# Attention outputs turned in 32-wide blocks on VectorE, with output weights laid out to match

## The chip, the cores and the metric

The kernel runs on one core of a Trainium2 chip. The metric is the device time of one execution in microseconds (us). The engines are TensorE (PE; its weight loads are shown as PEld), VectorE (DVE), ScalarE (ACT), GpSimd (POOL) and SyncE (SP), which mostly issues DMAs.

## What is computed

A transformer layer on x of shape (8, 256, 512), all in f32. `_layernorm` normalises rows; 32 query heads of width 16 share 8 key/value heads, so a *group* is 4 query heads with their key/value head.

```python
B, T, HID, H, HK, D = 8, 256, 512, 32, 8, 16
q = heads(concat([ctx, ln(x)]) @ Wq, 32)
kcat = concat([ctx @ Wsk, ln(x) @ Wk]); vcat = concat([ctx @ Wsv, ln(x) @ Wv])
scores = q @ kcat.T / sqrt(D) + alibi      # each token sees the 64 before it, twice
o = softmax(scores) @ vcat                 # per head, D = 16
x = x + tanh(g_xattn) * (o.reshape(B, T, HID) @ Wo)
n = ln(x)
# feed-forward: router softmax, top 4 of 128, experts as mixtures of 8 bases,
# and a shared gated product
x = x + tanh(g_ffn) * ffn(n)
```

## The kernel before

Every f32 operand of a large product is split into a high and a low part of type fp32r, and a product is three passes (hi x hi, lo x hi, hi x lo; `PASSES`, `product` at L1509).

Attention is software-pipelined over slots. A slot `n` is one block of 64 queries of one group of one batch: 4 blocks (NB) x 8 groups (HK) = 32 slots a batch (UNITS), 256 slots (END) in all and 38 more that drain the pipeline. Each engine's program is a loop over the slots, in which offsets (L75 to L82) say how many slots after its own first slot a piece of work is done: `due(n, offset)` for work once a batch, `group_due(n, offset)` for work once a group. The order on each engine is fixed by hand; engines meet at semaphores.

In slot n TensorE computes the scores of slot n (`scores`, L1594, into one of two banks; it waits until VectorE has the maxima of slot n-2), then the turned scores of slot n-14 (`scores_turned`, L1615; ScalarE takes their exponentials, L867). VectorE takes the row maxima (`maxima`, L1180). Once a group TensorE turns the maxima's halves (`turn_max`, L1605), which ScalarE copies and sends into the query stack by a DMA.

With the values (`times_v`, L1628) come 128 rows by 256 tokens in `PO`: for each of 4 heads 32 rows, of which 16 are the output and 16 hold the sum of exponentials (the values are followed by ones). Then:

- ScalarE copies `PO` to `OS` (`pv_out`, L875), which frees `PO` for the next group.
- TensorE turns `OS` in two 128x128 turns (`turn_o`, L1639) into `PN`: tokens by (head, 32).
- VectorE takes the reciprocal of the sums (L1196) and multiplies (L1200) into `O`, rows of tokens by 512 (`norm`). It stands before the slot's maxima.
- Once a batch, TensorE turns `O` back in 2 x 4 turns (`turn_rows`, L1646); ScalarE and VectorE split it into `OT` hi and lo (`rows_high` L881, `rows_low` L1206).
- Two products with Wo (`times_wo`), the residual, statistics (`residual`, L1215 to L1220), roots on GpSimd (`x1_roots`), normalisation (`x1_normalise`, L1226), turns of x (`turn_x`, L1658), and its split (`x_high` L885, `x_low` L1231), which for the first six batches uses the memory of `OT` and is kept in HBM by a DMA (L558).

All projections, turns of inputs, rows, Wo products and turns of x share two PSUM banks (`PJ`) in the order of `projections()` (L122): a job waits until VectorE is done with the job two before it (`take_bank`). In slots modulo 32 the jobs stand at: inputs 0, 1, 2, 3; K 5, 6; queries 8, 10, 12, 14; turn of V 16; rows 21, 22; Wo 24, 26; V 28, 29; x 31 and 0 (`rows`, `wo` and `x` belong to the batch before). After the 256 slots the first tiles of the feed-forward are interleaved with the drain (`ROUTER_AT`, `SHARED_AT`); the feed-forward follows.

## Time and profile before

| | us |
|---|---|
| median of 3 runs | 999.35 |
| lowest, highest | 998.37, 1000.41 |
| profiled execution | 1003.41 |
| its span, first to last instruction | 1001.6 |
| TensorE busy | 934.7 |
| VectorE busy | 567.5 |
| ScalarE busy | 422.1 |
| GpSimd busy | 369.4 |

The busy times are those of the profiled execution, as the union of an engine's instructions. Matmuls overlap: the duration of one includes its latency, so the time that it takes from the engine is the distance from its start to the next one's. The attention slots run from about 40 to 460 us of the span, the drain to about 535, the feed-forward to the end.

### The profile page before, as it was taken

The page shows a single profiled execution, that of the slowest core. Times are in us where ns is not written, and L with a number is a line of the kernel's source. Part 1 is how long each engine was busy: PE and PEld are TensorE (multiplying, and loading weights), DVE is VectorE, ACT ScalarE, POOL GpSimd, SP SyncE. Part 2 cuts the span into 40 slices and gives each one's busy share as a digit, 9 for nine tenths or more (in the row PEclk, how much of TensorE's full clock was granted, in tenths as well). Part 3 has the DMA queues.
Part 4 walks back from the last instruction along what each step waited for, and adds up shares of the span by engine and source line. Part 5 has one row for each costly group of instructions (what it writes and reads, how often), then busy time and mean ns, then how long its engine had stood idle before and what let it go on. Part 6 is the DMA issues. An engine that isn't in the chain of part 4 may idle for free.

```text
span 1001.6 us, 18083 instructions
## 1 busy us (share of the span) xinstructions
PE 934.7 (93%) x6936; PEld 803.3 (80%) x6936; DVE 567.5 (57%) x1135; ACT 422.1 (42%) x906; POOL 369.4 (37%) x401
## 2 busy tenths in 40 slices
PE   6779999999999999999997988979999999999997
PEld 6668989888888989978786766768888888888876
DVE  5356574856657474666123564566566565565566
ACT  5655454444544444455311423334434444444331
POOL 2020000100000010002000997626687887887730
PEclk9989999999999999989999998989999999999998
DMA  6595566555655554698010104441111211201044
GB/s 219 167 204 154 125 165 162 150 178 137 175 141 162 130 156 124 159 248 255 1 42 1 43 22 156 150 158 41 65 51 39 79 40 45 85 26 59 22 151 185
DMA packets 79559, 117.04 MB, mean 117 GB/s; under 512 B 6249, under 2 KB 49002, under 8 KB 78442
## 3 DMA queue, kind: packets, MB, share of 16 engines
q1 hardware_dynamic: 77744, 115.18, 40.8%
q8 instruction: 56, 0.92, 0.4%
q10 hardware_dynamic: 1730, 0.71, 0.3%
q14 instruction: 29, 0.24, 0.1%
HBM read 77.13 MB, written 37.81 MB: 115 GB/s over the span
## 4 chain that ended last, share of the span: by engine, by line
PE 84%; DVE 7%; DMA 4%; issue 2%; ACT 1%; SPq 1%; POOL 0%; DVEq 0%; ACTq 0%; POOLq 0%
PE ps_proj L1515 21%; PE ps_scores L1840 17%; PE ps_scoresT L1840 9%; PE ps_scores L1515 5%; PE ps_o L1628 5%; PE ps_scoresT L1615 5%; PE ps_scores L1594 4%; PE ps_proj L1840 4%; PE ps_scoresT L1515 4%; PE ps_o_max L1639 2%; DVE neg_max L1180 1%; PE ps_proj L1538 1%; PE ps_o L1515 1%; DMA xn_rows<-in_x 1%; DMA q_kept<-qT_hi 1%
## 5 line engine op out<-in xcount | busy, mean ns | idle before, releaser
L1180 DVE TENSOR_REDUCE neg_max<-ps_scores 128x2 f32<-128x384 f32 (+1 forms) x256 | 130.4, 517 | 127.3 <-PE ps_scores L1594 126.4
L867 ACT ACTIVATE probsT<-ps_scoresT 128x512 f32<-128x512 f32 (+1 forms) x256 | 138.8, 544 | 144.3 <-PE ps_scoresT L1615 140.8
L1071 ACT ACTIVATE part_sums<-ps_scores 128x512 f32<-128x512 f32 x96 | 57.5, 599 | 134.3 <-PE ps_scores L1840 132.4
L1594 PE MATMUL ps_scores<-k_stack,q_stack 114*128 114x192 f32 (+1 forms) x512 | 105.3, 291 | 9.0 <-DVE neg_max L1180 8.1
L1615 PE MATMUL ps_scoresT<-q_stack,k_stack 116*128 116x256 f32 x448 | 105.8, 308 | 6.2 <-DMA q_stack<-max_rows 4.9
L1594 PEld LDWEIGHTS ps_scores<-k_stack,q_stack 114*128 114x128 f32 x512 | 81.7, 197 | 17.0 <-DVE neg_max L1180 12.3
L650 POOL TENSOR_SCALAR var_eps<-mean_var 128x2 f32<-128x2 f32 x8 | 2.1, 261 | 226.9 <-DVE mean_var L1129 226.8
L765 POOL TENSOR_TENSOR big<-big,basis 128x512 f32<-128x512 f32 x56 | 77.5, 1403 | 15.6 <-DVE basis L1469 15.6
L753 POOL TENSOR_TENSOR w_expert_lo<-w_sums,w_expert_hi 128x256 fp32r<-128x256 f32 x64 | 64.2, 1014 | 46.9 <-ACT w_expert_hi L1001 46.9
L1615 PEld LDWEIGHTS ps_scoresT<-q_stack,k_stack 116*128 116x128 f32 x448 | 73.4, 199 | 7.9 <-DMA q_stack<-max_rows 5.3
L1515 PE MATMUL ps_proj<-actT_hi,wq_hi 128*128 128x256 f32 x224 | 65.1, 290 | 0.0
L1628 PE MATMUL ps_o<-probsT,v_ones 128*32 128x128 f32 (+1 forms) x2048 | 64.4, 268 | 0.5 <-issue 0.5
L1515 PE MATMUL ps_proj<-actT_hi,wq_lo 128*128 128x256 f32 x224 | 63.8, 285 | 0.0
L1515 PE MATMUL ps_proj<-actT_lo,wq_hi 128*128 128x256 f32 x224 | 63.8, 285 | 0.0
L650 POOL TENSOR_SCALAR x_var_eps<-x_mean_var 128x2 f32<-128x2 f32 x8 | 2.8, 354 | 161.1 <-DVE x_mean_var L1220 161.1
L1460 DVE TENSOR_TENSOR basis<-part_sums,silu_gate 128x512 f32<-128x512 f32 x32 | 24.0, 751 | 67.2 <-ACT silu_gate L1079 67.2
L1628 PEld LDWEIGHTS ps_o<-probsT,v_ones 128*32 128x32 f32 x2048 | 53.6, 112 | 10.0 <-issue 1.7
L1469 DVE TENSOR_TENSOR basis<-basis,big 128x512 f32<-128x512 f32 x56 | 58.2, 1040 | 1.0
L753 POOL TENSOR_TENSOR w_expert_lo<-w_raw,w_expert_hi 128x256 fp32r<-128x256 f32 x48 | 45.9, 968 | 20.3 <-ACT w_expert_hi L1001 20.2
L1439 DVE TENSOR_TENSOR part_sums<-part_sums,ps_scoresT 128x512 f32<-128x512 f32 x32 | 22.0, 688 | 54.0 <-ACT part_sums L1071 54.0
L1840 PE MATMUL ps_scores<-sum_hi,w_expert_hi 128*128 128x512 f32 x128 | 50.1, 392 | 2.1 <-ACT part_sums L1071 2.1
L1840 PE MATMUL ps_scores<-xnT_hi,w_expert_hi 128*128 128x512 f32 x128 | 49.9, 390 | 1.1 <-DVE x_part L1391 1.1
(264 smaller groups left out, 2571.5 us busy)
## 6 DMA issues: line engine op xcount, KB each, us to landing
k_stack<-k_kept SPq DMA_DIRECT2D x64, 192.0 KB, 5.3
q_stack<-q_kept SPq DMA_DIRECT2D x31, 384.0 KB, 5.4
q_kept<-qT_hi SPq DMA_DIRECT2D x16, 512.0 KB
big<-coeff_rows SPq DMA_DIRECT2D x8, 1024.0 KB, 4.7
xn_rows<-in_x SPq DMA_DIRECT2D x8, 512.0 KB, 4.0
k_kept<-kT_hi SPq DMA_DIRECT2D x16, 256.0 KB
q_kept<-qT_lo SPq DMA_DIRECT2D x8, 512.0 KB
x_rows<-in_x SPq DMA_DIRECT2D x8, 512.0 KB, 5.1
```

The source lines that it names most:

```text
L753: pool.tensor_tensor(WS[n % 2]["lo"][:, w, :], w_source(n, w), WS[n % 2]["hi"][:, w, :].bitcast(F32), ALU.subtract).then_inc(e_lo, 1)
L765: pool.tensor_tensor(dst, dst, BS[:, j, :], ALU.add).then_inc(acc_done, 1)
L867: act.activation(PT[:, g % 2, 2 * j:2 * j + blocks].rearrange("p h f r w -> p (h f r w)"), ST[:, n % 2, 0:blocks].rearrange("p h n -> p (h ...
L1071: act.activation(TP[:, u % 2, j, :], src[:, u % 2, :], ACT.Copy).then_inc(taken, 1)
L1180: dve.tensor_reduce(NM[:, g % 2, 2 * i:2 * i + 2], SA[:, n % 2, :, 0:keys], AX.X, ALU.max, negate=True).then_inc(max_done, 1)
L1460: dve.tensor_tensor(BS[:, j, :], up, silu, ALU.mult).then_inc(e_prod, 1)
L1469: dve.tensor_tensor(dst, BS[:, j, :], cB[:, k % 2, group_columns(t)], ALU.mult).then_inc(basis_done, 1)
L1515: ins = pe.matmul(out, stat(s, c), mov(m, c), start=c == cs[0] and j == 0, stop=c == cs[-1] and j == PARTS - 1)
L1594: ins = pe.matmul(SA[:, n % 2, f, 0:2 * (near.stop - near.start)], QS[0:TOP, g, i, f].rearrange("p r w -> p (r w)"), keys[:, near, :].rear ...
L1615: ins = pe.matmul(ST[:, n % 2, v, :], KS[0:ROWS, g, j + v, 1 - v].rearrange("p w s -> p (w s)"), QS[0:ROWS, g, j + v].rearrange("p f r w - ...
L1628: ins = pe.matmul(PO[32 * r:32 * r + 2 * D, j * W:j * W + cols_j], VA[:, j, g, :], PT[:, n % 2, 2 * j:2 * j + cols_j // W, :, r, :].rearra ...
L1840: ins = pe.matmul(bank[:, u % 2, :], WS[n % 2][s][:, w, c * P:(c + 1) * P], operand(MEETS[w], m, c, g), start=first and c == 0 and j == 0, ...
```

## The change

PO is turned by VectorE itself, straight out of PSUM, in 32x32 blocks (`o_turn`): the 32 rows of a head and 32 tokens become 32 tokens by 32. In that form it takes the reciprocal and multiplies; the 16 values of two neighbouring groups (an even and an odd one) are laid side by side, and at the odd one a second 32x32 turn brings them back as (head, group parity, 16) by tokens, `OR`. ScalarE and VectorE split `OR` into `OT` (`o_high`, `o_low`), once a pair of groups. The turns on TensorE (`turn_o`, `turn_rows`), the copy `pv_out` and the split of the rows are gone. `times_v` waits for VectorE's turn. The rows of Wo are permuted before the launch to match. x gets buffers of its own (`XS`; its low half is kept by two DMAs instead of one). `o_turn` stands behind the slot's maxima.

The jobs modulo 32 are now: inputs 0 to 3; K 5, 6; queries 8, 10, 13, 16; turn of V 15; Wo 20, 23; V 25, 27; x 30, 31. The last router product is in slot 33 of the drain instead of 34.

```diff
@@ -73,13 +73,12 @@
...
-NM_TURN, PV, PV_OUT, TURN_O, NORM = 6, LAG + 5, LAG + 6, LAG + 9, LAG + 10
-TURNS_BETWEEN = (TURN_O - NM_TURN) // NB
+NM_TURN, PV, O_TURN, O_HIGH, O_LOW = 6, LAG + 5, LAG + 6, LAG + 7, LAG + 8
...
-PREP, K_PROJ, Q_PROJ, V_PROJ = (-32, -31, -30, -29), (-27, -26), (-24, -22, -20, -18), (-4, -3)
+PREP, K_PROJ, Q_PROJ, V_PROJ = (-32, -31, -30, -29), (-27, -26), (-24, -22, -19, -16), (-7, -5)
...
-TURN_V, TURN_ROWS, TIMES_WO, TURN_X = 16, (53, 54), (56, 58), (63, 64)
-LOAD_X1, X1_ROOTS, X1_NORMALISE, KEEP_X = 42, 59, (62, 63), 67
+TURN_V, TIMES_WO, TURN_X = 15, (52, 55), (62, 63)
+LOAD_X1, X1_ROOTS, X1_NORMALISE, KEEP_X = 42, 57, (60, 61), 66
@@ -114,7 +113,7 @@
...
-ROUTER_AT = {0: 0, 4: 1, 12: 2, 34: 3}
+ROUTER_AT = {0: 0, 4: 1, 12: 2, 33: 3}
@@ -164,11 +163,13 @@
...
-    O = at("o_rows", 192 * KIB, [P, TB, HID])
-    OS = at("oT_sums", 196 * KIB, [P, T])
+    OB = at("o_blocks", 192 * KIB, [P, T // 32, 2 * D])
+    ON = at("o_normal", 193 * KIB, [P, 2, T // 32, 2 * D])
+    OR = at("oT_raw", 195 * KIB, [P, 2, T])
...
+    XS = {"hi": at("xs_hi", 216 * KIB, [P, HC, T], F32R), "lo": at("xs_lo", 208 * KIB, [P, TB, HC, P], F32R)}
@@ -554,9 +554,10 @@
...
-                for j, h in enumerate(("hi", "lo")):
-                    sp.dma_start(xT_kept_d[b, j].rearrange("p c n -> p (c n)"),
-                                 OT[h][:, :, :, :].rearrange("p t c n -> p (t c n)").bitcast(F32)).then_inc(xT_kept, 16)
+                sp.dma_start(xT_kept_d[b, 0].rearrange("p c n -> p (c n)"),
+                             XS["hi"][:].rearrange("p c n -> p (c n)").bitcast(F32)).then_inc(xT_kept, 16)
+                for t in range(TB):
+                    sp.dma_start(xT_kept_d[b, 1][:, :, t * P:(t + 1) * P], XS["lo"][:, t].bitcast(F32)).then_inc(xT_kept, 16)
@@ -868,20 +869,18 @@
...
-        def pv_out(n):
-            act.wait_ge(pv_mm, n + 1)
-            if n >= 1:
-                act.wait_ge(o_turned, n)
-            act.activation(OS[:], PO, ACT.Copy).then_inc(oT_out, 1)
-        def rows_high(b, t):
-            act.wait_ge(oT_mm, TB * b + t + 1)
-            if t == 0 and 1 <= b <= SPILLED:
-                act.wait_ge(xT_kept, 32 * b)
-            act.activation(OT["hi"][:, t], chunks(place("rows", b, t)), ACT.Copy).then_inc(oT_hi, 1)
+        def o_high(p):
+            b, c = divmod(p, HC)
+            act.wait_ge(o_back, p + 1)
+            if c == 0 and b >= 1:
+                act.wait_ge(wo_mm, TB * b)
+            act.activation(OT["hi"][:, :, c, :], OR[:, p % 2, :].rearrange("p (t n) -> p t n", t=TB), ACT.Copy
+                           ).then_inc(oT_hi, 1)
...
         def x_high(b, t):
...
+            if t == 0 and 1 <= b < SPILLED:
+                act.wait_ge(xT_kept, 48 * b)
...
         def split_hi(idx, used=None):
@@ -1189,22 +1185,30 @@
...
-        def norm(n):
-            b, g = divmod(n, HK)
+        def o_turn(n):
+            p, odd = divmod(n, 2)
+            dve.wait_ge(pv_mm, n + 1)
+            if n >= 1:
+                dve.wait_ge(o_done, n)
+            dve.transpose(OB[:].rearrange("p k e -> p (k e)"), PO).then_inc(o_turned, 1)
...
-            v = PN.rearrange("p (t r e) -> p t r e", t=TB, r=G)
-            dve.reciprocal(RI[:], v[:, :, :, D]).then_inc(inv_done, 1)
-            if g == 0 and b >= 1:
-                dve.wait_ge(oT_mm, TB * b)
+            dve.reciprocal(RI[:], OB[:, :, D]).then_inc(inv_done, 1)
...
-            dve.tensor_tensor(O[:, :, g * G * D:(g + 1) * G * D].rearrange("p t (r d) -> p t r d", r=G),
-                              v[:, :, :, 0:D], RI[:].unsqueeze(3).broadcast_to([P, TB, G, D]),
-                              ALU.mult).then_inc(o_done, 1)
-        def rows_low(b, t):
-            dve.wait_ge(oT_hi, TB * b + t + 1)
-            dve.tensor_tensor(OT["lo"][:, t], chunks(place("rows", b, t)),
-                              OT["hi"][:, t].bitcast(F32), ALU.subtract).then_inc(pj_done, 1)
+            dve.tensor_tensor(ON[:, p % 2, :, odd * D:(odd + 1) * D], OB[:, :, 0:D],
+                              RI[:].unsqueeze(2).broadcast_to([P, T // 32, D]), ALU.mult).then_inc(o_done, 1)
+            if odd:
+                dve.wait_ge(o_done, n + 1)
+                if p >= 2:
+                    dve.wait_ge(oT_lo, p - 1)
+                dve.transpose(OR[:, p % 2, :], ON[:, p % 2].rearrange("p k e -> p (k e)")).then_inc(o_back, 1)
+        def o_low(p):
+            c = p % HC
+            dve.wait_ge(oT_hi, p + 1)
+            dve.tensor_tensor(OT["lo"][:, :, c, :], OR[:, p % 2, :].rearrange("p (t n) -> p t n", t=TB),
+                              OT["hi"][:, :, c, :].bitcast(F32), ALU.subtract).then_inc(oT_lo, 1)
...
         def residual(b, t):
@@ -1223,6 +1227,8 @@
...
+            if t == 0 and 1 <= b <= SPILLED:
+                dve.wait_ge(xT_kept, 48 * b)
@@ -1269,11 +1275,14 @@
...
-            m = group_due(n, NORM)
-            if m is not None:
-                norm(m)
+            m = group_due(n, O_LOW)
+            if m is not None and m % 2:
+                o_low(m // 2)
...
+            m = group_due(n, O_TURN)
+            if m is not None:
+                o_turn(m)
@@ -1600,8 +1606,6 @@
...
-            if n > TURNS_BETWEEN:
-                pe.wait_ge(o_done, n - TURNS_BETWEEN)
...
         def scores_turned(n):
@@ -1621,7 +1625,7 @@
...
-                pe.wait_ge(oT_out, n)
+                pe.wait_ge(o_turned, n)
@@ -1630,25 +1634,9 @@
...
-        def turn_o(n):
-            pe.wait_ge(oT_out, n + 1)
-            if n >= 1:
-                pe.wait_ge(o_done, n)
-            pe.wait_ge(nm_out, min(n + TURNS_BETWEEN + 1, GROUPS))
-            for t in range(TB):
-                ins = pe.transpose(PN[:, t * P:(t + 1) * P], OS[:, t * P:(t + 1) * P], ident[:])
-            ins.then_inc(o_turned, 1)
-        def turn_rows(b, t):
-            dst = take_bank("rows", b, t)
-            pe.wait_ge(o_done, HK * (b + 1))
-            for c in range(HC):
-                ins = pe.transpose(dst[:, c * P:(c + 1) * P], O[:, t, c * P:(c + 1) * P], ident[:])
-            ins.then_inc(oT_mm, 1)
         def times_wo(b, t):
...
-            pe.wait_ge(pj_done, passed("rows", b, t))
+            pe.wait_ge(oT_lo, HC * (b + 1))
...
         def turn_x(b, t):
@@ -1927,6 +1908,8 @@
...
+    heads = inputs["L0_xattn_Wo"].reshape(HK // 2, 2, G, D, HID)
+    inputs["L0_xattn_Wo"] = np.asarray(heads).transpose(0, 2, 1, 3, 4).reshape(HID, HID)
```

## Rows read from the trace of the kernel before

**Rows 1.** Page, part 1: engine, busy us (share of the span), instructions.

```profile
PE 934.7 (93%) x6936; PEld 803.3 (80%) x6936; DVE 567.5 (57%) x1135; ACT 422.1 (42%) x906; POOL 369.4 (37%) x401
```

**Rows 2.** Timeline, TensorE: start, us, engine, line, operation, tiles; where slots and K begin.

```profile
256.28 0.42 PE L1594 MATMUL ps_scores<-k_stack,q_stack 114*128 114x128 f32 x2
...
265.42 0.35 PE L1515 MATMUL ps_proj<-actT_hi,wkv_hi 128*128 128x256 f32 x1 [0.70 <-DVE actT_lo L1145]
...
297.04 0.42 PE L1594 MATMUL ps_scores<-k_stack,q_stack 114*128 114x128 f32 x2
...
305.67 0.42 PE L1594 MATMUL ps_scores<-k_stack,q_stack 114*128 114x128 f32 x2
...
312.11 0.42 PE L1594 MATMUL ps_scores<-k_stack,q_stack 114*128 114x128 f32 x2
...
369.52 0.42 PE L1594 MATMUL ps_scores<-k_stack,q_stack 114*128 114x128 f32 x2
```

**Rows 3.** Groups by line and form, TensorE: records, busy us, mean ns, idle before.

```profile
L1639 PE MATMUL ps_o_max<-ident,oT_sums 128*128 128x128 f32 x128 | 28.2, 302 | 0.0
```

**Rows 4.** Timeline, TensorE, same columns: prices from start to start.

```profile
293.90 0.63 PE L1646 MATMUL ps_proj<-ident,o_rows 128*128 128x128 f32 x4
294.29 0.45 PE L1594 MATMUL ps_scores<-k_stack,q_stack 114*128 114x192 f32 x2
...
295.94 0.97 PE L1628 MATMUL ps_o<-probsT,v_ones 128*32 128x128 f32 x32
296.84 0.44 PE L1639 MATMUL ps_o_max<-ident,oT_sums 128*128 128x128 f32 x2
...
297.58 0.40 PE L1515 MATMUL ps_proj<-wo_hi,oT_hi 128*128 128x512 f32 x1
...
300.35 0.37 PE L1594 MATMUL ps_scores<-k_stack,q_stack 114*128 114x192 f32 x2
...
306.21 0.28 PE L1515 MATMUL ps_proj<-actT_hi,wkv_hi 128*128 128x256 f32 x1
...
307.65 0.37 PE L1594 MATMUL ps_scores<-k_stack,q_stack 114*128 114x192 f32 x2
...
308.00 0.28 PE L1515 MATMUL ps_proj<-actT_hi,wkv_hi 128*128 128x256 f32 x1
```

**Rows 5.** Groups by line and form, VectorE: same columns.

```profile
L1200 DVE TENSOR_TENSOR o_rows<-ps_o_max,inv_sums 128x128 f32<-128x128 f32 x64 | 18.7, 292 | 2.7
...
L1157 DVE TENSOR_TENSOR qT_lo<-ps_proj,qT_hi 128x256 fp32r<-128x256 f32 x28 | 11.6, 416 | 3.7 <-ACT qT_hi L847 3.7
```

**Rows 6.** Timeline, VectorE: the start behind the scores, and the residual.

```profile
300.75 0.56 DVE L1180 TENSOR_REDUCE neg_max<-ps_scores 128x2 f32<-128x384 f32 x1 [2.22 <-PE ps_scores L1594]
301.23 0.74 DVE L1215 SCALAR_TENSOR_TENSOR x_rows<-ps_proj,tanh_gates,x_rows 128x512 f32<-128x512 f32 x1
...
302.83 0.53 DVE L1180 TENSOR_REDUCE neg_max<-ps_scores 128x2 f32<-128x384 f32 x1
```

**Rows 7.** Timeline, VectorE, light groups of the last batch.

```profile
434.18 0.21 DVE L1196 RECIPROCAL inv_sums<-ps_o_max 128x8 f32<-128x8 f32 x1 [0.97 <-PE ps_o_max L1639]
...
434.63 0.41 DVE L1180 TENSOR_REDUCE neg_max<-ps_scores 128x2 f32<-128x256 f32 x1
...
437.89 0.21 DVE L1196 RECIPROCAL inv_sums<-ps_o_max 128x8 f32<-128x8 f32 x1 [0.97 <-PE ps_o_max L1639]
```

**Rows 8.** Timeline, TensorE: a turn of inputs that waited in slot 1.

```profile
373.32 0.66 PE L1538 MATMUL ps_proj<-ident,ctx_rows 128*128 128x128 f32 x4 [1.11 <-DVE actT_lo L1145]
```

**Rows 9.** Windows: us, busy of each engine (count), PEclk, DMA share, GB/s.

```profile
370.00:374.00 4.00, 2.34 (x19) 1.91 (x19) 3.16 (x8) 2.52 (x6) 0.00 (x0) 0.99 0.10 17
374.00:378.00 4.00, 4.00 (x46) 3.57 (x46) 2.31 (x4) 2.54 (x5) 0.00 (x0) 0.58 0.78 302
```

**Rows 10.** Timeline, TensorE: the turns of x after the last batch.

```profile
528.23 1.08 PE L1658 MATMUL ps_proj<-ident,x_normal 128*128 128x128 f32 x8 [1.40 <-DVE x_normal L1226]
```

More of the change, by code:

```diff
@@ L127, in projections @@
     kinds = [("prep", PREP, 2), ("k", K_PROJ[1:], 2), ("q", Q_PROJ, 1), ("v", V_PROJ[1:], 1), ("turn_v", (TURN_V,), 0),
-             ("rows", TURN_ROWS, 0), ("wo", TIMES_WO, 0), ("x", TURN_X, 0)]
+             ("wo", TIMES_WO, 0), ("x", TURN_X, 0)]
     for n in range(SLOTS):
@@ L225, in build @@
     gates, tg = little("gates", [P, 2]), little("tanh_gates", [P, 2])
-    RI = little("inv_sums", [P, TB, G])
+    RI = little("inv_sums", [P, T // 32])
     amp, amp2, mix = little("amp", [P, KB, 2]), little("amp2", [P, KB]), little("mix", [P, KB])
@@ L243, in build @@
     PNM = ps("ps_o_max", [P, 2, T])
-    PO, PN, PM = POB[:, 0, :], PNM[:, 0, :], PNM[0:4 * NB, 1, 0:P]
+    PO, PM = POB[:, 0, :], PNM[0:4 * NB, 1, 0:P]
     PG = SA[:, :, :, :].rearrange("p s h n -> p s (h n)")
@@ L265, in build @@
         sem("s_mm"), sem("max_done"), sem("nm_hi"), sem("nm_lo"), sem("nm_t"), sem("nm_out"))
-    st_mm, exp_done, pv_mm, oT_out, o_turned, inv_done, o_done = (
-        sem("st_mm"), sem("exp_done"), sem("pv_mm"), sem("oT_out"), sem("o_turned"), sem("inv_done"), sem("o_done"))
-    oT_mm, oT_hi, wo_mm, x1_st, x1_ag, x1_rt, x1_n = (
-        sem("oT_mm"), sem("oT_hi"), sem("wo_mm"), sem("x1_st"), sem("x1_ag"), sem("x1_rt"), sem("x1_n"))
+    st_mm, exp_done, pv_mm, o_turned, inv_done, o_done, o_back = (
+        sem("st_mm"), sem("exp_done"), sem("pv_mm"), sem("o_turned"), sem("inv_done"), sem("o_done"), sem("o_back"))
+    oT_hi, oT_lo, wo_mm, x1_st, x1_ag, x1_rt, x1_n = (
+        sem("oT_hi"), sem("oT_lo"), sem("wo_mm"), sem("x1_st"), sem("x1_ag"), sem("x1_rt"), sem("x1_n"))
     xT_mm, xT_hi, x1_kept, xT_kept = sem("xT_mm"), sem("xT_hi"), sem("x1_kept"), sem("xT_kept")
@@ L361, in xT_place @@
         if b < SPILLED:
-            return OT[h][:, :, :, :].rearrange("p t c n -> p (t c n)").rearrange(
-                "p (c t n) -> p c t n", c=HC, t=TB)[:, :, t, :]
+            return XS[h][:, :, t * P:(t + 1) * P] if h == "hi" else XS[h][:, t]
         return XT[h][:, :, (b * TB + t) * P:(b * TB + t + 1) * P]
@@ L568, in _ @@
                 sp.wait_ge(pj_done, passed("v", B - 1, 0))
-                sp.wait_ge(xT_kept, 32 * (m + 1))
+                sp.wait_ge(xT_kept, 48 * (m + 1))
                 sp.dma_start(XT[("hi", "lo")[j]][:, :, m * T:(m + 1) * T].bitcast(F32), xT_kept_d[m, j]).then_inc(xT_in[m // 2], 16)
@@ L947, in _ @@
             for t in range(TB):
-                b = due(n, TURN_ROWS[t] + 1)
-                if b is not None:
-                    rows_high(b, t)
                 b = due(n, TURN_X[t] + 1)
@@ L970, in _ @@
                 act.activation(tg[:], gates[:], ACT.Tanh).then_inc(tg_done, 1)
-            m = group_due(n, PV_OUT)
-            if m is not None:
-                pv_out(m)
+            m = group_due(n, O_HIGH)
+            if m is not None and m % 2:
+                o_high(m // 2)
             s = n - (END - UNITS)
             if s == 18:
-                split_hi(0)
+                split_hi(0, (xT_kept, 48 * SPILLED))
             if s == 20:
@@ L1271, in _ @@
         for n in range(SLOTS):
-            m = group_due(n, NORM)
-            if m is not None:
-                norm(m)
+            m = group_due(n, O_LOW)
+            if m is not None and m % 2:
+                o_low(m // 2)
             if n < END:
                 maxima(n)
+            m = group_due(n, O_TURN)
+            if m is not None:
+                o_turn(m)
             for i in range(4):
@@ L1294, in _ @@
             for t in range(TB):
-                b = due(n, TURN_ROWS[t] + 1)
-                if b is not None:
-                    rows_low(b, t)
                 b = due(n, TIMES_WO[t] + 1)
@@ L1726, in _ @@
                 times_v(m)
-            m = group_due(n, TURN_O)
-            if m is not None:
-                turn_o(m)
             for i in range(4):
@@ L1752, in _ @@
                 turn_v(b)
-            for t in range(TB):
-                b = due(n, TURN_ROWS[t])
-                if b is not None:
-                    turn_rows(b, t)
             for t in range(TB):
```

## Prediction, before the result was known

> **What bounds the kernel now.** I read the page's busy times first: TensorE is busy 93% of the span, VectorE 57%, ScalarE 42% [rows 1]. That is an average, so I went on to the timeline of TensorE's instructions in the attention stage (40 to 505 us), where the change lies. Each slot there starts with the scores matmuls of L1594, so their starts are the slot clock, and a batch is 32 slots. In batch 4 (counted from 0) slots 0 to 4 and the head of 5 take 9.14 us (256.28 to 265.42), slots 5 to 23 take 31.62, slots 24 to 27 take 8.63, slots 28 to 31 take 6.44: together 55.83 us [rows 2]. I split the batch there because three of the four stretches have different limits. The groups by form name what is removed: the turns of L1639 have 128 records, 28.2 us of busy time [rows 3]. A busy time isn't a price here, as matmuls overlap. The price is the distance to the next start.
>
> **What the change takes from TensorE.** A pair of turns (L1639) holds it from 296.84 to 297.04, 0.20 us; four turns of rows (L1646) from 293.90 to 294.29, 0.39 us [rows 2, 4]. There are 64 pairs and 16 fours: 12.8 + 6.2 = 19.0 us. That is the most that TensorE alone can give back, and it counts only where TensorE sets the pace.
>
> **What it adds to VectorE.** Before, a group of heads costs a reciprocal and a product, 0.45 us from start to the next instruction (434.18 to 434.63) [rows 7], and 16 subtractions for the rows. After, a group costs a turn of 128x256 out of PSUM, the reciprocal, the product, and each second group another turn back; each pair of groups also a 128x256 subtraction. No turn on VectorE is in the trace. The nearest row is the 128x256 subtraction out of PSUM, 416 ns [rows 5]; the turn also moves 256 elements per partition. Its bounds: below, 0.20 us, what the product of half the width needs before the next starts (0.292 us long [rows 5]); above, twice the subtraction, 0.83. I take 0.42, and 0.45 where the next waits for it. An even group is then 0.45 + 0.45 = 0.90 us. An odd one must let the product end (0.12 more) and adds 0.33 for the turn back: 1.35. It is placed behind the slot's own maxima, and queued behind it on VectorE are the low halves of projections, the residual, the halves of the maxima, and the next maxima, for which the scores two slots on wait. ScalarE loses a 128x256 copy per group and the rows' copies and gains one copy per pair; it is under half busy and I cost it at nothing, with its slots' exponentials as cover.
>
> The Trainium skill, VectorE: DVE Perf Modes, "The three transpose paths", gives 311 ns for VectorE's 128x128 in blocks of 32 against 390 ns for TensorE's. By those figures TensorE's pair would be 0.78 us and the change would gain about 0.1 us a group even if VectorE were the bound; this trace has 0.20 us for the pair from start to start, so the page's durations are no exchange rate here.
>
> **The sum, batch by batch.** Prices in TensorE's time [rows 4]: a slot of scores and turned scores 0.54 (305.67 to 306.21) or 0.35 where only one turned block is due (307.65 to 308.00); 0.90 more with the values (295.94 to 296.84); a K or V half 1.44 (306.21 to 307.65), so a query part 2.88; a pass through Wo 2.77 (297.58 to 300.35). On average four bare slots are 2.8 with the values.
> Slots 5 to 23 afterwards: 4 fours 11.2, slots 6 and 7 1.95, K 2.88, four query parts 11.5, the turn of V 0.39, two passes of Wo that came from slots 24 and 26 5.54: 33.5. VectorE falls behind a little at slots 19, 20 and 23 (slot 16 has an odd group, the values' copy and statistics): 0.9. So 34.4, from 31.62.
> Slots 24 to 27: after the scores of 24 VectorE starts 0.40 later (300.35 to 300.75) and does maxima 0.34, an odd group 1.35, the residual with its statistics 1.60 (301.23 to 302.83) [rows 4, 6], halves 0.34, and only then the maxima of slot 25, 0.56. Scores of slot 27 can't start before 4.6; slot 27 itself is 1.44 + 1.44. In all 7.5, from 8.63. V now sits there, Wo doesn't.
> Slots 28 to 31: VectorE does maxima, an even group, the copy of V, a normalisation and the halves before TensorE can turn the first block of x: 3.2 us after the scores of 28. Then 0.39, and slot 31 with values and the second turn 1.8. In all 5.3, from 6.44.
> Slots 0 to the K half in 5: one projection a slot over two banks; now x's last low half (0.60) is behind an odd group, so the second turn of the inputs waits until about 3.0 us after the scores of 0; slots 2 and 3 cost 1.1 and 1.9; slot 4 has an even group ahead of the last low half, so K starts 1.8 after slot 5's scores; today TensorE already idles 0.70 before it (the row at 265.42) [rows 2]. In all 8.9, from 9.14.
> Sum 34.4 + 7.5 + 5.3 + 8.9 = 56.1 against 55.83: the 2.4 us that TensorE loses in work come back as waits for VectorE. Six batches: +1.8.
> The last batch has no projections. Its light groups take 3.71 us (434.18 to 437.89) with VectorE waiting 0.97 of them [rows 7]. There the chain runs maxima, scores, values, scores, maxima. The norm's 0.45 leaves it and 0.90 or 1.35 enters: some 4.1 and 4.5. Five such groups: +3.0; elsewhere in that batch three pairs and one set of rows are saved: -1.4. After it, where TensorE runs the shared products: four pairs 0.8, the last rows 0.8, and the wait of 1.40 for the normalised x [rows 10], which now has two shared tiles ahead of it instead of one: -3.0. First batch: -0.2. Total +1.8 + 1.6 - 3.0 - 0.2 = +0.2 us. The profiled execution is 1003.41 us with a span of 1001.6; it would be 1003.6. The shown runs have a median of 999.35, 4.1 below it, so I predict 999.6.
> On SP's queue the queries' store moves two slots later (-16 to -14 before the batch), the first read of them, at -10, waits for it, and they are used at slot 0: ten slots hide it, and without them it would be one landing. The x blocks get places of their own and one more DMA in 512-byte rows for six batches; queued behind it there are stacks that are fetched 14 slots ahead, so nothing. If that cover failed it would be one landing per batch, some 4 us in all.
>
> **Rivals.** (1) VectorE's extra work stays hidden. For it: it's idle 43% of the time, and the one-job-a-slot spread breaks the chain in which TensorE waited 1.11 us for a low half in slot 1 [rows 8]. If half of the 19.0 us stays, 990; if all of it, 980. Against it: the waits computed above at slots 27, 30 and 1. (2) More slow clock. In 370 to 374 us TensorE was busy 2.34 of 4 us, and in the next four the granted clock was 0.58, near the lower of its levels, 1.2 GHz [rows 9]. Such a batch took 57.41 us (312.11 to 369.52) against 55.83 [rows 2], so 1.6 us each, and it's not in every batch. The new waits spread over slots 24 to 5 and are longer in total, some 6 us; if three or four more of them fall, that is 5 to 6 us: 1005. It decides from the point where stretches around slot 1 are as empty as this one. The Trainium skill, TensorE: Matmul & The Clock Gate, Part 1, says that the array is run at half rate after idleness; the two rows agree. (3) The turn of four-byte data costs twice: 0.41 more each, six turns on the path of a batch, 2.5 us; with the last batch +16, of which some hides: 1012. Against it: every other pass over 256 elements takes about 0.42. (4) The change doesn't give TensorE time at all, because the turns that go were in gaps that stay (at the end, too, where the 3.0 us of the sum would then not come): 999.35 + 0.2 + 3.0, so 1002.5. Against it: between 295.94 and 297.04 TensorE goes from the values to the turns to the scores with no idle time noted [rows 2, 4].
>
> **How the numbers follow.** The forecast, stretched to whatever ends within 0.2% (2 us, about what a measurement of this kernel can tell from none), 0.32. (1) 0.31, with anything else that ends below that. (2) 0.20, (3) 0.10, (4) 0.07. Faster 0.31, same 0.32, slower 0.37. The range leaves out the far end of (1), where over half of the 19.0 us stays, and that of (3): 988 to 1011. Cases of both signs hold most of it; the likeliest one's own range is 997 to 1002.
>
> **What would show it.** The turn of 128x256 at 0.42 us on VectorE. A batch without slow clock at 55 to 57 us from scores to scores. TensorE waiting for maxima at slot 27 (over 1 us), for the normalised x at slot 30, for a low half at slot 1, and for VectorE before K. Light groups of the last batch at 4.1 and 4.5 us. VectorE's busy time up by about 64 x 0.42 + 32 x 0.42 + 32 x 0.42 less 11, some 43 us. Wrong if light groups stay at 3.7, or if batches come in at 53 us: then VectorE isn't in the way; or at 59, then a turn costs more than I took.

## The result, and the profile after

The changed kernel takes 1019.26 us (median of four runs, 1013.49 to 1023.81); the kernel before, in the same series, 998.86. The ratio is 1.019, interval 1.0147 to 1.0232: slower by 19 to 20 us. I had forecast 999.6, with a range up to 1011. The profiled execution of after is 1018.43 us, its span 1016.6. The one of before was among its longer ones (1003.41 against a median of 999.35), so the traces show 15.0 of these 20 us.

The page's busy line of after, as in [rows 1]:

```profile
PE 927.8 (91%) x6744; PEld 789.7 (78%) x6744; DVE 604.3 (59%) x1247; ACT 409.5 (40%) x858; POOL 369.9 (36%) x401
```

TensorE has 192 matmuls fewer and is busy 6.9 us less, VectorE 36.8 us more. VectorE's new groups by line and form, against [rows 3, 5]:

```profile
L1195 DVE STREAM_TRANSPOSE o_blocks<-ps_o 128x256 f32<-128x256 f32 x64 | 28.2, 440 | 9.8 <-PE ps_o L1632 9.8
...
L1199 DVE TENSOR_TENSOR o_normal<-o_blocks,inv_sums 128x128 f32<-128x128 f32 x64 | 18.7, 292 | 2.2
...
L1205 DVE STREAM_TRANSPOSE oT_raw<-o_normal 128x256 f32<-128x256 f32 x32 | 14.3, 445 | 1.1
L1210 DVE TENSOR_TENSOR oT_lo<-oT_raw,oT_hi 128x256 fp32r<-128x256 f32 x32 | 13.2, 412 | 2.5 <-ACT oT_hi L877 2.5
```

The turn takes 0.44 us; I had taken 0.42. The whole of an even group holds VectorE for 0.92 us (375.25 to 376.17), that of an odd one for 1.40 (367.56 to 368.96), where I had 0.90 and 1.35. So the prices were right. Now the slot clock, as in [rows 2]: starts of TensorE's scores in batch 5 of after (slots 0, 24, 28, and 0 of the next), and its K half.

```profile
322.62 0.42 PE L1600 MATMUL ps_scores<-k_stack,q_stack 114*128 114x128 f32 x2
...
325.53 0.66 PE L1544 MATMUL ps_proj<-ident,ctx_rows 128*128 128x128 f32 x4 [1.43 <-DVE xs_lo L1237]
...
331.78 0.36 PE L1521 MATMUL ps_proj<-actT_hi,wkv_hi 128*128 128x256 f32 x1 [1.50 <-DVE actT_lo L1141]
...
366.84 0.34 PE L1600 MATMUL ps_scores<-k_stack,q_stack 114*128 114x128 f32 x2
...
370.97 0.28 PE L1609 MATMUL ps_o_max<-ident,max_halves 128*16 128x128 f32 x1 [1.25 <-DVE max_halves L1185]
...
374.53 0.34 PE L1600 MATMUL ps_scores<-k_stack,q_stack 114*128 114x128 f32 x2
...
377.64 0.28 PE L1609 MATMUL ps_o_max<-ident,max_halves 128*16 128x128 f32 x1 [1.23 <-DVE max_halves L1185]
...
380.08 0.42 PE L1600 MATMUL ps_scores<-k_stack,q_stack 114*128 114x128 f32 x2
```

This batch, in which no slow clock falls, takes 57.46 us; the like one before took 55.83 [rows 2]. TensorE has less to do in it and waits four times for VectorE: for x's low half before the turn of the inputs in slot 1, for the last low half before K, and twice for the halves of the maxima (slots 26 and 30). These last waits are the new ones. All waits of TensorE over 0.15 us in this batch (total us, times, longest):

```profile
PE ps_o_max L1609 <- DVE max_halves L1185: 2.5, 2, 1.3
PE ps_proj L1521 <- DVE actT_lo L1141: 1.5, 1, 1.5
PE ps_proj L1544 <- DVE xs_lo L1237: 1.4, 1, 1.4
PE ps_scores L1600 <- DVE neg_max L1176: 0.6, 2, 0.4
```

Together 6.0 us; in the like batch before they are 3.0 (0.55 before the second turn of x in slot 0, 1.11 in slot 1, 0.70 before K, 0.68 before the scores of slot 19). Outside these waits TensorE takes 52.8 us of the batch before and 51.5 after, 1.3 less, where the turns that are gone had been priced at 2.4.

TensorE's waits in the whole execution, before and then after (same columns):

```profile
PE ps_scores L1594 <- DVE neg_max L1180: 8.1, 16, 1.3
PE ps_proj L1538 <- DVE actT_lo L1145: 6.7, 8, 1.1
...
PE ps_o_max L1605 <- DVE max_halves L1189: 3.0, 1, 3.0
```

```profile
PE ps_o_max L1609 <- DVE max_halves L1185: 22.5, 20, 2.2
PE ps_proj L1521 <- DVE actT_lo L1141: 10.5, 7, 1.5
PE ps_proj L1544 <- DVE xs_lo L1237: 7.1, 5, 1.4
PE ps_scores L1600 <- DVE neg_max L1176: 7.0, 22, 1.3
```

What stands ahead of the halves is seen in VectorE's timeline, slot 24 of the same batch:

```profile
368.27 0.29 DVE L1199 TENSOR_TENSOR o_normal<-o_blocks,inv_sums 128x128 f32<-128x128 f32 x1
368.60 0.45 DVE L1205 STREAM_TRANSPOSE oT_raw<-o_normal 128x256 f32<-128x256 f32 x1
368.96 0.71 DVE L1219 SCALAR_TENSOR_TENSOR x_rows<-ps_proj,tanh_gates,x_rows 128x512 f32<-128x512 f32 x1
369.71 0.69 DVE L1222 BATCH_NORM_STATS2 x_stats<-x_rows 128x6 f32<-128x512 f32 x1
370.44 0.18 DVE L1224 BATCH_NORM_AGGREGATE x_mean_var<-x_stats 128x2 f32<-128x6 f32 x1
370.53 0.15 DVE L1183 CAST max_halves<-neg_max 128x8 fp32r<-128x8 f32 x1
370.72 0.19 DVE L1185 TENSOR_TENSOR max_halves<-neg_max,max_halves 128x8 fp32r<-128x8 f32 x1
370.83 0.55 DVE L1176 TENSOR_REDUCE neg_max<-ps_scores 128x2 f32<-128x384 f32 x1
```

Turn, reciprocal, product and turn back, then the residual with its statistics, then the halves, and only then the maxima of slot 25. VectorE has no gap from the maxima of slot 24 (367.22) to those of slot 25. It is 3.99 us from the scores of slot 24 to the maxima of slot 25 (366.84 to 370.83). TensorE's own work covers 2.88 of them (slots 24, 25 and the scores of 26, up to 369.72, where its wait of 1.25 begins).

Where the 15.0 us of span went, from the starts of the scores: first batch +1.1; batch 1 +4.4 (53.88 to 58.29); the next five +6.9; the last batch, from its first to its last scores, +6.4 (39.72 to 46.13); from there to the end -3.8 (535.9 to 532.1). The last batch also runs into the slow clock, one window of it:

```profile
446.00:450.00 4.00, 4.00 (x34) 3.34 (x36) 2.81 (x9) 2.33 (x5) 0.00 (x0) 0.50 1.09 318
```

The granted clock (column before the last two) is 0.50, the lower of the two levels.

Over the whole execution the mean granted clock is 0.971 before and 0.966 after. With two levels that is 58 us at the lower one before and 69 after. What they cost is an estimate: a batch before whose mean is 0.97 takes 1.6 us more than one at 1.00, so a microsecond at the lower level costs about half of one. The 11 more are then worth about 5 of the 15.0 us.

### The profile page after: what moved, and what is told of

Same layout as the page of the kernel before. It is cut to its first block, busy times and chain, and to the rows that moved or that the text cites. A ratio compares the mean times of both kernels' runs of the same rounds, so it can differ in the third digit from the quotient of the medians.

```text
span 1016.6 us, 17719 instructions
## 1 busy us (share of the span) xinstructions
PE 927.8 (91%) x6744; PEld 789.7 (78%) x6744; DVE 604.3 (59%) x1247; ACT 409.5 (40%) x858; POOL 369.9 (36%) x401
## 4 chain that ended last, share of the span: by engine, by line
PE 78%; DVE 13%; issue 3%; DMA 3%; ACT 1%; SPq 1%; POOL 0%; DVEq 0%; POOLq 0%; ACTq 0%
PE ps_proj L1521 19%; PE ps_scores L1821 17%; PE ps_scoresT L1821 9%; PE ps_o L1632 6%; PE ps_scores L1521 5%; PE ps_scores L1600 5%; PE ps_proj L1821 4%; PE ps_scoresT L1521 4%; PE ps_scoresT L1619 4%; DVE o_blocks L1195 2%; DVE neg_max L1176 2%; PE ps_o L1521 1%; DMA xn_rows<-in_x 1%; DVE actT_lo L1141 1%; PE ps_proj L1544 1%
## 5 line engine op out<-in xcount | busy, mean ns | idle before, releaser
L868 ACT ACTIVATE probsT<-ps_scoresT 128x512 f32<-128x512 f32 (+1 forms) x256 | 135.2, 542 | 148.4 <-PE ps_scoresT L1619 146.4
L1632 PE MATMUL ps_o<-probsT,v_ones 128*32 128x128 f32 (+1 forms) x2048 | 67.7, 277 | 0.5 <-issue 0.5
L1632 PEld LDWEIGHTS ps_o<-probsT,v_ones 128*32 128x32 f32 x2048 | 56.2, 116 | 10.6 <-issue 2.4
L1445 DVE TENSOR_TENSOR part_sums<-part_sums,ps_scoresT 128x512 f32<-128x512 f32 x32 | 22.0, 688 | 55.7 <-ACT part_sums L1067 55.7
```

The costliest lines, as they stand in the source:

```text
L868: act.activation(PT[:, g % 2, 2 * j:2 * j + blocks].rearrange("p h f r w -> p (h f r w)"), ST[:, n % 2, 0:blocks].rearrange("p h n -> p (h ...
L1632: ins = pe.matmul(PO[32 * r:32 * r + 2 * D, j * W:j * W + cols_j], VA[:, j, g, :], PT[:, n % 2, 2 * j:2 * j + cols_j // W, :, r, :].rearra ...
```

## Experiments

A "place" is a slot modulo 32. Every ratio is to the kernel before, run beside it. "Clean batch" is one without slow clock, from scores to scores: 55.83 us before, 57.46 after; it and all waits and windows are of the profiled execution. In the diffs, lines in parentheses stand for a call that is shortened. The kernel before has medians from 997.8 to 1000.6 us in these series, so a difference between runs of two series is good to 2 or 3 us; where it matters, the difference by the ratios is given too.

### e1: the change with the old places

```diff
-... (-24, -22, -19, -16), (-7, -5)
+... (-24, -22, -20, -18), (-4, -3)
-TURN_V, TIMES_WO, TURN_X = 15, (52, 55), (62, 63)
+TURN_V, TIMES_WO, TURN_X = 16, (54, 56), (63, 64)
```

X1_ROOTS, X1_NORMALISE, KEEP_X and the router's slot go back as well.

> The changed kernel with the jobs placed as before (queries 8, 10, 12, 14, turn of V 16, V 28 and 29, x 31 and 0, last router product 34; Wo at 22 and 24, two slots earlier than before, since the rows' turns are gone). Theory 1, VectorE's longer chain per group is what costs: it stays at or above the changed kernel, 1018 to 1028 us, since x's two turns and an input's meet an odd group in slot 0 again. Theory 2, the new places cost, the turns don't: back to 998 to 1004 us.

1034.69 us, ratio 1.0357 (1.0323 to 1.0392). The new places aren't what loses the time: without them the change is 15 us worse. That is 7 us above the range that I gave for theory 1; the mean granted clock is 0.955 here and 0.966 in after.

### e2: the new places without the change

```diff
-... (-24, -22, -20, -18), (-4, -3)
+... (-24, -22, -19, -16), (-7, -5)
-TURN_V, TURN_ROWS, TIMES_WO, TURN_X = 16, ...
+TURN_V, TURN_ROWS, TIMES_WO, TURN_X = 15, ...
```

> The kernel before, its turns on TensorE, with only the places of the projections that can move alone: queries 8, 10, 13, 16, turn of V 15, V 25 and 27. Theory 1: within 3 us of the kernel before, and a clean batch at 54 to 57 us (55.8 before). Theory 2: slower by 8 us or more.

1010.82 us, 1.0121 (1.0071 to 1.0171); a clean batch 57.22. The trace names the reason, a collision that the change doesn't have, since Wo stays at 24 and 26 here and V at 25 takes a PSUM bank that the residual still reads (a wait of one batch):

```profile
PE ps_proj L1515 <- DVE x_rows L1215: 1.2, 1, 1.2
```

By its range (8 us or more) this was theory 2, and the clean batch was just above the 54 to 57 us of theory 1. But the wait is one of its own, so this run says that places matter by 12 us, and little on the change itself.

### e3: turns of an eighth of the size

```diff
-dve.transpose(OB[:].rearrange("p k e -> p (k e)"), PO)
+dve.transpose(OB[:, 0], PO[:, 0:32])
-dve.transpose(OR[:, p % 2, :], ON[:, p % 2].rearrange("p k e -> p (k e)"))
+dve.transpose(OR[:, p % 2, 0:32], ON[:, p % 2, 0])
```

Seven eighths of the attention outputs are left out.

> The changed kernel, but each turn on VectorE covers 32 of the 256 columns, so 7/8 of the attention outputs are left out; instructions, waits and order stay. Each of the 96 turns gets about 0.23 us shorter (0.44 to about 0.21). Theory 1: on a path of six turns a batch that is 1.4 us a batch, and 0.23 or 0.46 a light group, so 9 to 12 us less than the changed kernel: 1007 to 1010 us. Theory 3, the wait for TensorE's slow clock is what costs and VectorE's price is hidden: within 3 us of the changed kernel.

1004.3 us, 1.0058 (1.0031 to 1.0085): 15 us less than after (13 by the ratios; I had 9 to 12), and 1.4 us less in a clean batch (56.05). The turns' time on VectorE is on the path. It isn't all of the loss: with turns that cost half of that, the change is still slower than the kernel before.

### e4: the turn at the end of its slot, behind the halves

```diff
-            m = group_due(n, O_TURN)
-            if m is not None:
-                o_turn(m)
             ...
                 max_halves(m)
+            m = group_due(n, O_TURN)
+            if m is not None:
+                o_turn(m)
```

> The changed kernel with VectorE's group work put behind the low halves, the copy of V, the residual, the normalisation and the halves of the maxima of its slot, right behind the halves. Theory 1 with the place as the cause (what is queued behind the group's work makes TensorE wait): the waits for halves, for x's low half in slot 1 and before K go, 1.2 to 1.5 us each, four a batch of which the next maxima take back half: 1003 to 1010 us. If only the amount of VectorE's work counts: within 3 us of the changed kernel.

1021.01 us, 1.0218 (1.0182 to 1.0253): no better than after, as the second theory had it. The one clean batch is 0.6 us shorter (56.86), but the other batches have slow clock in them (mean of the execution 0.960), and the last one takes 49.0 us instead of 46.1. The waits changed their name (total us, times, longest, whole execution):

```profile
PE ps_scores L1600 <- DVE neg_max L1176: 26.0, 29, 1.6
...
PE ps_o_max L1609 <- DVE max_halves L1185: 4.7, 8, 1.9
```

### e5, e6: the turn two slots later, turn back three

```diff
-NM_TURN, PV, O_TURN, O_HIGH, O_LOW = 6, LAG + 5, LAG + 6, LAG + 7, LAG + 8
+NM_TURN, PV, O_TURN, O_BACK, O_HIGH, O_LOW = 6, LAG + 5, LAG + 8, LAG + 9, LAG + 10, LAG + 11
-TURN_V, TIMES_WO, TURN_X = 15, (52, 55), (62, 63)
+TURN_V, TIMES_WO, TURN_X = 15, (54, 56), (62, 63)
```

e6 also has V at its old places, 28 and 29.

> The changed kernel with VectorE's group work moved and split: the turn, reciprocal and product two slots later (slots 2 modulo 4, behind the maxima, where VectorE is about to wait for the values), the turn back one slot after that, and Wo two slots and one slot later (22, 24). Same instructions, same amount. Theory 1a, the amount of work on VectorE costs: within 4 us of the changed kernel, light groups 4.3 us and more. Theory 1b, the work costs because it stands between the scores that follow the values and the halves, low halves and maxima that TensorE waits for: light groups at 3.5 to 3.8 us, a clean batch at 54 to 55.5 us, 995 to 1003 us.

> As e5, with V at slots 28 and 29 as in the kernel before. Theory 1b with the second cause (V's products used to cover the wait for the normalised x): a clean batch 1.0 to 2.0 us shorter than in e5, 985 to 997 us in all. If V's place doesn't count: as e5 within 3 us.

1006.34 us, 1.0061 (1.0031 to 1.0092), and 1006.96, 1.0056 (1.0026 to 1.0085). Moving the turn wins 13 us. That is less than theory 1b had (995 to 1003 us, a clean batch at 54 to 55.5; it is 56.47). Too late has a price too: TensorE now waits before the next values for the turn of the group before (e5).

```profile
PE ps_o L1637 <- DVE o_blocks L1195: 14.6, 24, 1.8
```

The places of V make no difference to the time that can be told here. A clean batch of e6 is 0.5 us shorter (55.98; I had 1 to 2), but slow clock falls in four of its batches 1 to 6, against two in e5.

### e7: fewer turns on TensorE in the kernel before

```diff
-            for t in range(TB):
+            for t in range(TB if n == 0 else 1):
                 ins = pe.transpose(PN[...
-            for c in range(HC):
+            for c in range(1):
                 ins = pe.transpose(dst[...O[...
```

One of two turns of each group and three of four turns of the rows are left out.

> The kernel before with one instead of two turns of the attention outputs per group, and one instead of four turns of rows, so most of its attention outputs are wrong; VectorE's and ScalarE's work stays. TensorE loses 63 times 0.10 and 48 times 0.10 us, 11 us of work in all. If TensorE's turns are on its path, as my sum said: 6 to 11 us less than before, 988 to 993 us. If they fill gaps that stay: within 3 us of before.

994.45 us, 0.9927 (0.9883 to 0.997), 1.5 us above the range; a clean batch 54.80 instead of 55.83. TensorE's turns are on its path, so their time can be had, but not all of it: 14 turns a batch at 0.10 us are 1.4, and 1.03 come back.

### e8, e9, e10: halves first, turn later

e8 makes the halves right behind the maxima, and puts the turn one slot later at the end of the slot, with the turn back behind it:

```diff
-NM_TURN, PV, O_TURN, O_HIGH, O_LOW = 6, LAG + 5, LAG + 6, LAG + 7, LAG + 8
+NM_TURN, PV, O_TURN, O_BACK, O_HIGH, O_LOW = 6, LAG + 5, LAG + 7, LAG + 7, LAG + 8, LAG + 9
             if n < END:
                 maxima(n)
+            (max_halves of NM_TURN - 2)
             ...
-            (max_halves of NM_TURN - 2)
+            (o_turn, o_turn_back)
```

e9 adds `V_PROJ = (-7, -6)` and `STATS = (-51, -48)`. e10 is the kernel before with the halves moved alone.

> The changed kernel with three things moved on VectorE's queue and nothing left out: the halves of the maxima are made right behind the maxima of their slot, ahead of all low halves; the turn of a group's outputs stands one slot later (a slot in which no halves are due) and at the end of that slot, with the turn back directly behind it; ScalarE's copy and the low half follow one slot later each. VectorE's work stays the same. Theory A (the changed kernel lost its gain because the transposes of 0.44 us stand ahead of what TensorE waits for next: halves in the light slots, low halves elsewhere): the waits for max_halves (4.5 us a batch in the steady batches, 7.7 us in the last) and for xs_lo (1.4 us) go, a steady batch takes 53 to 55 us instead of 57.5, the last one 3 to 5 us less, in all 980 to 998 us. Theory B (VectorE simply has too much to do in some slots, wherever the turn stands): the waits come back under other names, 1005 to 1020 us.

> As the run before it, and in addition the second half of the value projection one slot earlier (places 25 and 26 of a batch, instead of 25 and 27), and the row statistics of the query input at places 13 and 16 instead of 16 and 17. If slot 26, then with no work but scores, was a place where TensorE waited for VectorE or fell to the slow clock, a steady batch gains 0.5 to 1 us over the run before it (975 to 992 us in all); if not, the two runs agree within 0.3%.

> The kernel before with one thing moved: the halves of the maxima right behind the maxima, ahead of the low halves and the residual. Theory A says that the kernel before hardly waits for the halves (no wait for max_halves over 0.6 us is seen in its steady batch), so that this is worth at most 0.5 us a batch there: 994 to 1000 us. If it gains as much as the same move gains in the changed kernel, the place of the halves was a flaw of both kernels and not what the change brought in.

1005.03 us, 1.0034 (1.0012 to 1.0055); 1003.29, 1.0031 (1.0002 to 1.006); 1002.26, 1.0031 (0.9999 to 1.0063). e8 comes out as theory B had it (1005 to 1020 us), though its last batch is 4.8 us shorter than in after, as A had it: no wait for the halves is left in a steady batch, but in slot 23 TensorE waits for the turn, which is now behind the residual. e9 agrees with e8 within 0.3%. That doesn't show that V's second half and the statistics do nothing: a clean batch is 0.85 us shorter in e9 (55.85 against 56.70), about what I had expected, and its first batch 5.6 us longer (53.9 against 48.3, at a granted clock of 0.81 against 0.89). The longest waits of one steady batch of e8:

```profile
PE ps_scores L1605 <- DVE neg_max L1176: 1.5, 2, 1.3
PE ps_o L1637 <- DVE o_blocks L1195: 1.5, 2, 1.3
PE ps_proj L1526 <- DVE actT_lo L1141: 1.2, 1, 1.2
```

e10 is 2 us above what was expected and no gain, so the place of the halves wasn't a flaw of the kernel before.

### e11, e12: the turn right behind the maxima, one slot later

e11 is e9 with `o_turn` directly behind `maxima` and `max_halves`; only the turn back stays at the end of the slot. e12 has the fourth turn of the inputs at place 4 and K at 6 and 7 as well.

```diff
             (max_halves of NM_TURN - 2)
+            (o_turn)
             ...
-            (o_turn, o_turn_back)
+            (o_turn_back)
```

> The run e9 with one thing moved: the turn of a group's outputs, with reciprocal and division, directly behind the maxima of its slot (ahead of the low halves and the residual) instead of at the slot's end; the turn back stays at the end. In e9 a steady batch still waits 1.7 us for this turn (three times) and 1.3 us for maxima behind it. If only the place costs, the first wait goes and a steady batch takes 54.0 to 55.3 us instead of 55.9, in all 985 to 999 us; if VectorE is simply full in these slots, the wait moves to low halves or maxima and the time stays at 1001 to 1006 us.

> As e11, and in addition the fourth turn of the inputs at place 4 instead of 3 of a batch and the key projection at 6 and 7 instead of 5 and 6, so that VectorE's four low halves do not stand in four slots in a row ahead of the projection that waits for them (1.2 us a batch for actT_lo in e9). If that wait is a matter of place, it goes: 0.6 to 1.2 us a batch less than e11, 4 to 9 us in all; if not, the same as e11 within 0.3%.

e11: 991.02 us, 0.9926 (0.9904 to 0.9948), faster than both kernels. A batch takes 54.47 us. Both lie where I had them if only the place costs. The only step from e9 is the turn's place in its slot, and it is worth 12 us (10 by the ratios). e12: 996.9, 0.9976 (0.9951 to 1.0001); slots 3 to 7 take 9.7 us of a batch instead of 8.8. That wait wasn't a matter of place, and my expectation of e12 was wrong.

### e13, e14, e15: one move at a time

e13 moves the halves alone to behind the maxima. e14 moves the turn, by one line; ScalarE's copy and the low half of the outputs follow it:

```diff
-NM_TURN, PV, O_TURN, O_HIGH, O_LOW = 6, LAG + 5, LAG + 6, LAG + 7, LAG + 8
+NM_TURN, PV, O_TURN, O_HIGH, O_LOW = 6, LAG + 5, LAG + 7, LAG + 8, LAG + 9
```

e15 has both.

> The changed kernel with the halves of the maxima made right behind the maxima of their slot (ahead of the turn, the low halves and the residual), and nothing else moved. The changed kernel waits 22.5 us for max_halves in 20 places. If these waits are a loss by themselves, they go and 14 to 22 us with them: 998 to 1005 us. If they only stand in front of other work of VectorE that TensorE needs just as soon, 1010 to 1019 us.

> The changed kernel with the turn, ScalarE's copy and the low half of the outputs one slot later each, so that the turn falls in slots in which no halves are due; nothing else moved. If the coincidence of the turn and the halves in one slot is the cause, this does as much as moving the halves ahead (998 to 1005 us); if the cause is that the halves stand behind low halves and the residual too, it gives back part of it: 1005 to 1014 us.

> Both moves, with the value projection at places 25 and 27 and the row statistics at 16 and 17 as in the changed kernel. If these last two do not matter, the same as e11 within 0.3% (988 to 994 us); if they cost what e9 against e8 let expect (0.2%), 990 to 996 us; above 998 us the value projection or the statistics are a cause of their own.

e13: 1039.88 us, 1.04 (1.0342 to 1.0459). e14: 995.3, 0.998 (0.9957 to 1.0004). e15: 996.94, 0.9989 (0.9963 to 1.0015). One slot later, and 24 us are back (21 by the ratios), more than either theory gave e14; the halves, moved ahead alone, cost 20 more, which neither theory allowed for. A clean batch of e14 takes 55.7 us, 1.7 less than in after, but only 0.1 less than in the kernel before: the change then costs nothing, and wins nothing that can be told. Both together do no more than the turn alone, 1 us beyond what I expected of e15. In e13 no wait for the halves stands among the waits of a steady batch, but the waits behind them do:

```profile
PE ps_scores L1600 <- DVE neg_max L1176: 2.0, 2, 1.6
PE ps_proj L1521 <- DVE actT_lo L1141: 1.8, 1, 1.8
PE ps_proj L1544 <- DVE xs_lo L1237: 1.7, 1, 1.7
PE ps_proj L1646 <- DVE x_normal L1232: 1.2, 1, 1.2
```

The rest of e13 is clock. Windows from the start of batch 1 to the last scores (same columns as [rows 9]), after, e13, e14:

```profile
90.20:484.50 394.30, 351.52 (x3868) 314.81 (x3861) 268.90 (x724) 166.25 (x379) 25.55 (x76) 0.97 0.61 157
```

```profile
93.10:509.10 416.00, 369.03 (x3864) 332.29 (x3861) 269.69 (x724) 163.95 (x379) 27.55 (x76) 0.91 0.57 149
```

```profile
89.60:464.00 374.40, 342.99 (x3865) 307.72 (x3861) 267.37 (x721) 166.45 (x377) 26.37 (x76) 0.99 0.63 164
```

With two levels, a mean of 0.91 means 18% of 416 us at the lower one, about 75 us; 0.97 means 24, 0.99 means 7. VectorE's busy time is the same in all three (267 to 270 us). The work hasn't changed; where it stands decides how long TensorE idles (stretch less PE busy: 43 us in after, 47 in e13, 31 in e14) and how much of the time it has the lower clock. At half a microsecond for each at the lower level, the clock is all of what e13 loses against after, and about half of what e14 wins; this is an estimate, no run holds the clock fixed.

Slots 24 and 25 in e14, VectorE's timeline:

```profile
358.96 0.18 DVE L1224 BATCH_NORM_AGGREGATE x_mean_var<-x_stats 128x2 f32<-128x6 f32 x1
359.06 0.15 DVE L1183 CAST max_halves<-neg_max 128x8 fp32r<-128x8 f32 x1
359.25 0.19 DVE L1185 TENSOR_TENSOR max_halves<-neg_max,max_halves 128x8 fp32r<-128x8 f32 x1
359.36 0.55 DVE L1176 TENSOR_REDUCE neg_max<-ps_scores 128x2 f32<-128x384 f32 x1
359.83 0.43 DVE L1195 STREAM_TRANSPOSE o_blocks<-ps_o 128x256 f32<-128x256 f32 x1
360.30 0.20 DVE L1197 RECIPROCAL inv_sums<-o_blocks 128x8 f32<-128x8 f32 x1
```

The maxima of slot 25 start 2.62 us after the scores of slot 24 (356.74), where in after it is 3.99 (366.84 to 370.83). The turn now stands behind them, and TensorE spends that time on slots 25 to 27, in which V is projected. Other waits stay or are new in e14: in the same batch 1.49 us before a turn of the inputs in slot 2 and 1.43 before the scores of slot 20.

## Why the prediction was wrong, point by point

| Part of the span, us | forecast | measured |
|---|---|---|
| first batch | -0.2 | +1.1 |
| batch 1 | +0.3 | +4.4 |
| the next five | +1.5 | +6.9 |
| last batch | +1.6 | +6.4 |
| behind it | -3.0 | -3.8 |
| sum | +0.2 | +15.0 |

The step that failed is the balance of a steady batch: that the waits for VectorE just eat up what TensorE gives back (56.1 us against 55.83). They come to more. With the like step for the last batch it makes up most of the error.

- **Price of the turn: right.** 0.42 taken, 0.44 measured, the turn back 0.445; with the rest of the group 0.92 and 1.40 against 0.90 and 1.35. Rival (3) falls. VectorE's busy time rose by 36.8 us; I had 43.
- **What TensorE gives back: right in kind.** e7 takes away part of the turns and wins 1.03 us per batch, of 1.4 by my price. Rival (4) falls.
- **A steady batch: the step that failed, by its size.** By the rows of batch 5: slots 0 to K 9.16 us (forecast 8.9), K to slot 23 35.06 (34.4), slots 24 to 27 7.69 (7.5), slots 28 to 31 5.55 (5.3). Together 57.46 instead of 56.1. The mechanism was seen, even the slots, and the waits weren't what was short: the turn in slot 1 came 2.91 us after the scores of 0 (3.0), K 2.00 after slot 5's (1.8), and between K and slot 24 the trace has one wait of 0.39 before slot 20 and values in slot 19 that take 1.36 instead of 0.90, together what I had (0.9). The rest of that stretch is TensorE's own pace, 34.2 us against the 33.5 of my sum: four bare slots take 2.9, not 2.8, a K half 1.51, not 1.44. So the waits came (3.0 to 6.0 us), and of the 2.4 us that were to pay for them only 1.3 show. With six batches an error of 1.4 us is worth 8.
- **The queues of slots 24 and 28: right.** The scores of slot 27 were to start 4.6 us after those of 24, and do (366.84 to 371.44); TensorE stops for it already in slot 26, at the turn of the maxima, which needs the halves, and not at the scores of 27. From the scores of 28 to the turn of x I had 3.2 us, measured 3.23 (374.53 to 377.76). There too TensorE stops at the turn of the maxima.
- **Batch 1.** I put +1.8 on six batches alike. Batch 1 takes 4.4 us more. By the starts of the slots, later batches win 0.9 us in slots 0 and 1 (4.2 to 3.3), where x's projections used to be waited for; batch 1 has nothing to win there (1.7 in both). Its slot 31 takes 3.36 us instead of 1.96, in the slow clock. With the 1.6 us of a clean batch that is 3.9 of the 4.4.
- **The last batch: the largest error of one batch, 6.4 us instead of 1.6.** Of its groups of four slots I had put the light ones at 4.1 and 4.5 us, from 3.7. By the starts of the slots, slots 8 to 11 take 4.9 us and 12 to 15 take 4.6; slots 0 to 7 take 12.4 (7.9 before), at a granted clock of 0.76 and then 0.50. Before, slots 12 to 19 weren't light either: 12.0 us, with a wait of 1.4 for a DMA and the clock at 0.55 in the last four, where after takes 9.8. The saving of 1.4 us that I had put against the light groups can't be told apart in this. My terms of 0.45 against 0.90 and 1.35 left out the wait for the halves (5.3 us in five places from 438 to 484 us) and the clock, at 0.50 for a time (the window above). In e14 this batch takes 41.3 us.
- **The end: right.** -3.8 against -3.0. **The first batch: wrong by 1.3 us**; no run says why.
- **Rival (1), hidden work, falls.** The three waits that I had against it came, in slots 26, 30 and 1.
- **Rival (2), slow clock,** had 0.20 and 5 to 6 us. In after it is a part, and about of that size (some 5 us, by the estimate above). In e13 it's the main part, so 5 to 6 us was no limit. In the direction of slower it was the right rival, but it comes on top of the forecast's own waits and isn't an alternative to them.
- **What I didn't see at all:** that with the turn one slot later the change costs nothing (e14). The diff puts it in slots that all have the halves of the maxima too, and one of them the residual (24), one the copy of V (28), one x's low half (0). I added the queue up for each of them and didn't ask whether the neighbouring slot had room.

Left open: why e13 falls into the slow clock so much more often than after, when its waits in a batch add up to about the same (6.7 us against 6.0). Also open is how the 6 us between e15 and e11 divide between V's second half, the statistics and the turn back: a clean batch is 1.4 us shorter in e11, and e8 and e9 put 0.85 of that to the first two together. And the low half of the outputs, which stands ahead of the maxima of its slot, moves with the turn in e14; no run moves one without the other, so its share isn't shown.

## What to carry to other kernels

When work moves from a full engine to one with room, add up the queue of the receiving engine slot by slot, against what the giving engine has to do in the same slots. If a slot comes out longer than its cover, try the next slot before judging the change. Reordering within the full slot didn't cure it: e4 renamed the waits, and e13 renamed them and lost 20 us more. What helped was to take the work out of the slot, to one where the other engine is busy (e14), close enough behind its input that its output isn't late (e5 was too late). In the slot with room the order counts again: behind the residual the turn came late (e8, e9), directly behind the maxima it won 10 to 12 us (e11). Sum up what the giving engine saves with the same care: here its own time, and not the waits, was most of the error in a steady batch.

## What the runs showed of the hardware

A turn of 128x256 of four bytes in 32x32 blocks takes VectorE 440 ns out of PSUM and 445 out of SBUF, as much as a subtraction of that size (412). A turn of an eighth of that takes 207 and 211 ns (e3), not an eighth of the time; over 96 turns that was worth 13 to 15 us. The clock granted in the attention stage went from 0.91 (e13) to 0.99 (e14) with the same instructions, by their order and place alone.

The Trainium skill, VectorE: DVE Perf Modes, "The three transpose paths", has 311 ns for VectorE's turn and 390 ns for TensorE's, both for 128x128 in bf16. No run here has that type. For four bytes and twice the width VectorE's turn takes 440 ns. For TensorE the duration isn't the price: it is 302 ns in the mean [rows 3], but a pair takes 0.20 us from start to start [rows 2, 4], and e7 wins 0.07 us for each turn left out.
